# Queries and keys projected in transposed form, with the rotary halves swapped by DMA

## The chip, the cores and the metric

The kernel runs on one core of a Trainium2 chip. The metric is the device time of one execution in microseconds. The engines are TensorE (PE, matmuls; its weight loads are shown apart as PEld), VectorE (DVE), ScalarE (ACT), GpSimd (POOL) and SyncE (SP, which only issues DMAs here). SBUF is the on-chip memory of 128 partitions, PSUM the small memory that PE writes.

## The reference

Four stages on 16 sequences of 256 tokens with 128 features, all in float32: a state-space layer, a mixture of experts, a second state-space layer, and a transformer of six layers. The change lies in the transformer's attention:

```python
qkv = x @ Wqkv                      # shift_tokens(x): half of the features come from the token before
q, k, v = jnp.split(qkv, 3, -1)     # 16 heads of 64
q = l2norm(q) * qs
k = l2norm(k) * ksc
q = q * cos * scale + rotate_half(q) * sin * scale     # rotate_half: [-x2, x1] of the two halves of a head
k = k * cos / scale + rotate_half(k) * sin / scale
out = local_attention(q, k, v)      # windows of 32 tokens; each looks at itself and the one before
out = out @ Wo
```

After it come a residual add, a layer norm and a feed-forward layer with a GELU.

## The kernel before

The transformer phase (`transformer_phase`) works on 96 pieces: 6 layers times 16 sequences, numbered n. It is a software pipeline with an order written out by hand. A pass m handles five pieces at once, in different stages: A = m is projected, rotated and its norms taken, R = m - 1 is normalised and turned and its values are projected, B = m - 2 does scores, softmax and attention, Dn = m - 3 finishes attention and its output projection (`combine`), C = m - 4 does the feed-forward part. F is the final norm of the last 16 pieces. Each engine has its own list of steps for a pass, in program order; semaphores join them. An engine that waits holds up everything behind it in its list, and the same goes for SP's queue of DMAs.

Queries and keys of a piece are four units u of 128x1024 float32: u // 2 says queries or keys, u % 2 which half of the tokens; j = 4n + u. In the kernel before:
- PE, `project(n, u)`: tokens on partitions, 1024 features (16 heads x 64) along the free axis, into PSUM tile `pQ`.
- ACT, `square`: squares of `pQ` into `sq`. DVE, `squares`: a sum over the 64 of each head, into `n2`.
- DVE, `rotate`: `rot` = pQ times the cosine table (L1364), `m2` = pQ with its halves swapped by the access pattern times the sine table (L1368). The tables `tabl` are rebuilt once a layer from `tab` and `rows` (L1330).
- DVE, `roots`: the reciprocal root of 64 sums per partition, an instruction at L1386 and then eleven small ones of 128x64 (L92 to L102).
- POOL, `rotary_add` (L1282): rot += m2. `unit_scale` (L1274): rot times the reciprocal root. `by_sum` (L1291): softmax probabilities times the reciprocal sum.
- PE, `turn` (L1707): eight 128x128 transposes of `rot` into the two PSUM banks `pM`. ACT, `turned`: copies to `qT` and `kT`, where the features are on partitions.
- PE, `scores` (L1634), `probs` (L1664), `attend` (L1683), `values` (L1718), `combine` (L1696), `hidden` (L1752).

POOL can't read PSUM here, so it works on SBUF alone. The ring `rot` has five buffers. A float32 matmul is two instructions on PE; a transpose is one. The experts' phase has two large products, on DVE (L639) and on POOL (L570).

## Time and profile before

| | |
|---|---|
| median of 3 runs | 4262.65 us (4262.21 to 4263.87) |
| profiled execution | 4261.88 us, its span 4260.1 us |
| busy: PE, DVE, ACT, POOL | 4080.9, 3309.8, 2401.9, 2222.1 us |
| mean granted PE clock | 0.985 of full |
| all DMAs | 186.16 MB, 44 GB/s in the mean |

The span is the time from the first to the last instruction in the profile. Busy times of different engines overlap. The transformer phase runs from about 980 us to the end.

### The profile page before, as it was taken

The page shows a single profiled execution, that of the slowest core. Times are in us where ns is not written, and L with a number is a line of the kernel's source. Part 1 is how long each engine was busy: PE and PEld are TensorE (multiplying, and loading weights), DVE is VectorE, ACT ScalarE, POOL GpSimd, SP SyncE. Part 2 cuts the span into 40 slices and gives each one's busy share as a digit, 9 for nine tenths or more (in the row PEclk, how much of TensorE's full clock was granted, in tenths as well). Part 3 has the DMA queues.
Part 4 walks back from the last instruction along what each step waited for, and adds up shares of the span by engine and source line. Part 5 has one row for each costly group of instructions (what it writes and reads, how often), then busy time and mean ns, then how long its engine had stood idle before and what let it go on. Part 6 is the DMA issues. An engine that isn't in the chain of part 4 may idle for free.

```text
span 4260.1 us, 144544 instructions
## 1 busy us (share of the span) xinstructions
PE 4080.9 (96%) x63655; PEld 2975.2 (70%) x63655; DVE 3309.8 (78%) x7007; ACT 2401.9 (56%) x4362; POOL 2222.1 (52%) x1342
## 2 busy tenths in 40 slices
PE   4999999886999999999999999999999999999997
PEld 3776776673777777777777777777777777777775
DVE  5434434456888888888888888888888888889995
ACT  1101110144677766777667766776767677666664
POOL 1101001025666666666666666666666666666662
PEclk8999999998999999999999999999999999999998
DMA  4111111000111111111111111111111111111110
GB/s 153 42 40 60 40 40 60 20 1 24 36 36 41 42 56 41 40 38 45 51 42 41 37 44 52 41 41 37 46 50 41 41 37 51 46 43 41 43 40 25
DMA packets 76231, 186.16 MB, mean 44 GB/s; under 512 B 15819, under 2 KB 44630, under 8 KB 71126
## 3 DMA queue, kind: packets, MB, share of 16 engines
q1 hardware_dynamic: 75606, 176.91, 13.5%
q8 instruction: 504, 8.26, 0.8%
q14 instruction: 121, 0.99, 0.1%
HBM read 61.25 MB, written 2.36 MB: 15 GB/s over the span
## 4 chain that ended last, share of the span: by engine, by line
PE 66%; DVE 5%; ACT 3%; issue 1%; POOL 1%; DMA 0%; POOLq 0%; DVEq 0%; SPq 0%
PE pQ L1650 15%; PE pTO L1683 9%; PE pS L1634 9%; PE pM L1718 7%; PE pTO L1696 7%; PE pM L1707 7%; PE pC L1752 6%; PE pTO L1664 3%; PE pC L1762 3%; ACT sq L1515 2%; ACT pS L1499 1%; DVE rot L1364 1%; DVE m L1368 1%; DVE n L1379 1%; POOL rot L1282 1%
## 5 line engine op out<-in xcount | busy, mean ns | idle before, releaser
L1282 POOL TENSOR_TENSOR rot<-rot,m 128x1024 f32<-128x1024 f32 x384 | 905.9, 2359 | 385.6 <-DVE m L1368 385.6
L1274 POOL TENSOR_TENSOR rot<-rot,rn 128x1024 f32<-128x1024 f32 x384 | 733.4, 1910 | 280.7 <-DVE rn L102 280.7
L1515 ACT ACTIVATE sq<-pQ 128x1024 f32<-128x1024 f32 x380 | 389.4, 1025 | 440.0 <-PE pQ L1650 439.8
L1291 POOL TENSOR_TENSOR E<-E,rc 128x512 f32<-128x512 f32 x384 | 401.3, 1045 | 348.0 <-DVE rc L1354 347.9
L1683 PEld LDWEIGHTS pTO<-PT,V 64*64 64x64 f32 x24576 | 402.3, 134 | 108.8 <-issue 100.1
L1364 DVE TENSOR_TENSOR rot<-pQ,tabl 128x1024 f32<-128x1024 f32 x380 | 457.0, 1203 | 12.5 <-ACT sq L1515 9.9
L1368 DVE TENSOR_TENSOR m<-pQ,tabl 128x1024 f32<-128x1024 f32 x380 | 461.5, 1215 | 0.1
L1634 PEld LDWEIGHTS pS<-kT,qT 64*32 64x32 f32 x24576 | 362.0, 107 | 142.1 <-issue 107.7
L1379 DVE TENSOR_REDUCE n<-sq 128x16 f32<-128x1024 f32 x380 | 459.4, 1209 | 0.0
L1634 PE MATMUL pS<-kT,qT 64*32 64x64 f32 x24576 | 427.2, 218 | 26.4 <-issue 16.9
L1683 PE MATMUL pTO<-PT,V 64*64 64x32 f32 x24576 | 444.4, 221 | 3.9 <-ACT PT L1524 2.5
L1707 PE MATMUL pM<-ident,rot 128*128 128x128 f32 x3072 | 416.7, 279 | 18.0 <-POOL rot L1274 13.5
L570 POOL TENSOR_TENSOR b_xcT<-b_cB,b_xT 128x2048 f32<-128x2048 f32 x16 | 72.3, 4517 | 691.8 <-DMA b_cB<-b_crow 691.8
L1532 ACT ACTIVATE oT<-pTO 128x256 f32<-128x256 f32 x768 | 252.7, 381 | 262.1 <-PE pTO L1683 262.0
L1650 PE MATMUL pQ<-wq,xs 128*128 128x512 f32 x760 | 380.3, 623 | 6.3 <-DVE m L1368 5.6
L1718 PE MATMUL pM<-wv,xs 128*128 128x512 f32 x768 | 362.3, 594 | 3.4 <-ACT XT L1486 3.4
L1707 PEld LDWEIGHTS pM<-ident,rot 128*128 128x128 f32 x3072 | 332.7, 141 | 38.8 <-POOL rot L1274 16.7
L1650 PE MATMUL pQ<-wk,xs 128*128 128x512 f32 x760 | 357.2, 592 | 0.8 <-DVE m L1368 0.8
L1696 PE MATMUL pTO<-oT,wo 128*128 128x256 f32 x1536 | 350.0, 381 | 0.6 <-ACT oT L1532 0.4
L1340 DVE TENSOR_REDUCE mx<-pS 128x8 f32<-128x512 f32 x384 | 262.7, 684 | 72.4 <-PE pS L1634 72.2
L1696 PEld LDWEIGHTS pTO<-oT,wo 128*128 128x128 f32 x1536 | 286.1, 191 | 37.0 <-ACT oT L1532 1.2
L1752 PE MATMUL pC<-xnT,w 128*128 128x256 f32 x1152 | 299.6, 383 | 4.0 <-DVE hh L1420 2.2
(229 smaller groups left out, 6967.6 us busy)
## 6 DMA issues: line engine op xcount, KB each, us to landing
V<-V SPq DMA_DIRECT2D x192, 384.0 KB, 3.5
b_cB<-b_crow SPq DMA_DIRECT2D x32, 1024.0 KB, 6.4
xs<-XT SPq DMA_DIRECT2D x192, 64.0 KB, 2.9
V<-V SPq DMA_DIRECT2D x96, 128.0 KB, 3.3
ys<-XT SPq DMA_DIRECT2D x192, 64.0 KB, 2.0
wq<-in_wqkv SPq DMA_DIRECT2D x6, 512.0 KB, 4.3
wk<-in_wqkv SPq DMA_DIRECT2D x6, 512.0 KB, 4.2
wv<-in_wqkv SPq DMA_DIRECT2D x6, 512.0 KB, 5.5
```

The costliest lines, as they stand in the source:

```text
L1274: e.tensor_tensor(r, r, rn[b % 2][:, c:c + HEADS].unsqueeze(2).to_broadcast([P, HEADS, HD]), ALU.mult)\
L1282: e.tensor_tensor(rot[j % RING][:, :], rot[j % RING][:, :], m2[:, :, :].rearrange("p h d -> p (h d)"), ALU.add)\
L1364: e.tensor_tensor(rot[j % RING][:, :].rearrange("p (h d) -> p h d", d=HD), projected(j)[:, :].rearrange("p (h d) -> p h d", d=HD), tl[:, t ...
L1368: e.tensor_tensor(m2[:, :, :].rearrange("p h (b d) -> p h b d", b=2), projected(j)[:, :].rearrange("p (h b d) -> p h b d", b=2, d=HD // 2) ...
L1379: e.tensor_reduce(n2[:, c:c + HEADS], squared(j).rearrange("p (h d) -> p h d", d=HD), AX.X, ALU.add)\
L1634: x = e.matmul(pS[32 * j:32 * j + 32, b * KEYS:(b + 1) * KEYS], q[r:r + HD, h // 2, WIN * w:WIN * (w + 1)], k[r:r + HD, h // 2, WIN * w:WI ...
L1650: x = e.matmul(projected(j)[:, i * 512:(i + 1) * 512], xs[n % 3][:, t * P:(t + 1) * P], wqkv[w][:, i * 512:(i + 1) * 512], start=True, sto ...
L1683: x = e.matmul(pOV[b % 2][c:c + HD, j // 2, w // 4, WIN * (w % 2):WIN * (w % 2 + 1)], V[n % 2][r:r + KEYS, w // 4, 1 - w % 2, h * HD:(h + ...
L1696: x = e.matmul(pO[:, 0:L], wo[:, c, :], oT[:, c, :], start=c == 0, stop=c == N // P - 1)
L1707: x = e.transpose(pM[i][:, c * P:(c + 1) * P], rot[j % RING][:, (4 * i + c) * P:(4 * i + c + 1) * P], ident[:, :])
L1718: e.matmul(pM[i][:, :], xs[n % 3][:, t * P:(t + 1) * P], wqkv[2][:, i * 512:(i + 1) * 512], start=True, stop=True)\
L1752: x = e.matmul(pC[:, a * L:(a + 1) * L], w1[:, c, :], xnT[:, :], start=True, stop=True)
```

## The change

Queries and keys are projected with the features on partitions and the 256 tokens along the free axis. A unit is now u // 2 = queries or keys and u % 2 = which eight heads, as four blocks of 128 features x 256 tokens. The transposes and their copies out of PSUM go away. In their place:
- ACT copies the unit from `pQ` to `rot` (`copied`), besides squaring it.
- Swapping the two halves of a head now means moving partitions: four DMAs on SP's queue (`swap`) copy `rot` to `rsw`, 32 partitions x 4 KB each.
- DVE multiplies `rot` by the cosine table in place (`cosine`) and `rsw` by the sine table in place (`sine`); POOL adds them as before.
- The sums of squares run over partitions, so PE takes them with a matrix of zeros and ones (`norms`, `sel`): 16 matmuls of 128x32 weights by 64 columns for a unit, into four 32-partition strips of the new PSUM tile `pN`. The matrix gives the 64 sums per partition a new layout.
- The reciprocal roots go to device memory (`write_rows`, `nrow`) and come back spread over partitions (`spread`, two DMAs of 64 partitions x 4 KB for a unit) into `rb`, and POOL's `unit_scale` multiplies `rot` by `rb`, writing to `qT` and `kT`.
- `pM` is one bank. The tables are transposed on PE at the start of the phase and their plain form is kept in device memory (`plain`), to be fetched again for each layer. `rot` has six buffers. The lists of all engines are reordered.

The diff, cut to its core:

```diff
-    RING = 5
+    RING = 6
...
+        plain = nc.dram_tensor("plain", (P, 4 * L), F32).ap()
+        tabl = [sb("tabl0", [P, 4 * L])[:, :], tab[:, :, :, :, :].rearrange("p t k i d -> p (t k i d)")]
+        tabl = [x.rearrange("p (k l) -> p k l", k=4) for x in tabl]
+        sel = sb("sel", [P, 16 * 32])
...
+        rb = [sb(f"rb{i}", [P, 4, L]) for i in range(2)]
+        nrow = [nc.dram_tensor(f"nrow{i}", (P, L // 4), F32).ap() for i in range(2)]
+        rsw = [sb(f"rsw{i}", [P, N]) for i in range(2)]
...
-        pM = [ps("pM0", [P, 512]), ps("pM1", [P, 512])]
+        pM = ps("pM", [P, 512])
+        pN = ps("pN", [P, 512])
...
+            def swap(n, u):
+                if n is None:
+                    return
+                j = 4 * n + u
+                e.wait_ge(a_raw.sem, a_raw.at("cp", j))
+                if j >= 2:
+                    e.wait_ge(g_add.sem, g_add.at("add", j - 2))
+                for a in range(4):
+                    b = a ^ 1
+                    e.dma_start(rsw[j % 2][a * HD // 2:(a + 1) * HD // 2, :], rot[j % RING][b * HD // 2:(b + 1) * HD // 2, :])\
+                        .then_inc(swap_l[j % 2], 16)
...
+            def write_rows(n):
+                if n is None:
+                    return
+                e.wait_ge(v_nt.sem, v_nt.at("rs", n))
+                if n >= 2:
+                    for i in range(2):
+                        e.wait_ge(rb_l[i], 32 * (2 * n - 3))
+                e.dma_start(nrow[n % 2], rn[n % 2][:, :]).then_inc(row_l, 16)
+            def spread(n, u):
+                if n is None or n == NP and u < 2 or n == 0 and u >= 2:
+                    return
+                i = 4 * (n - u // 2) + u
+                e.wait_ge(row_l, 16 * (n + 1))
+                if i >= 2:
+                    e.wait_ge(g_rn.sem, g_rn.at("rn", i - 2))
+                for x in range(2):
+                    src = nrow[n % 2].rearrange("(j i x) k -> i j (x k)", j=4, i=2)[x:x + 1, :, u * L:(u + 1) * L]
+                    e.dma_start(rb[u % 2][x * HD:(x + 1) * HD, :, :], src.to_broadcast([HD, 4, L])).then_inc(rb_l[u % 2], 16)
...
+                swap(A, 0)
+                N_ = A if A is not None else NP if R == NP - 1 else None
+                next_xs(A)
+                ffn_weights(C)
+                swap(A, 1)
+                write_rows(N_)
+                swap(A, 2)
+                spread(N_, 2)
+                spread(N_, 3)
+                next_ys(Dn)
+                swap(A, 3)
+                spread(N_, 0)
+                spread(N_, 1)
+                shift_values(R, 0)
+                store(F)
+                shift_values(R, 1)
...
-                b, c = n + u // 2, (u + 2) % 4 * HEADS
-                if u % 2 == 0:
-                    e.wait_ge(v_nt.sem, v_nt.at("rs", b))
+                e.wait_ge(rb_l[u % 2], 32 * (2 * n + u // 2 + 1))
+                if u % 2 == 0 and n >= 2:
+                    e.wait_ge(p_s.sem, p_s.at("s", 4 * (n - 2) + 3))
                 e.wait_ge(g_add.sem, g_add.at("add", j))
-                r = rot[j % RING][:, :].rearrange("p (h d) -> p h d", d=HD)
-                e.tensor_tensor(r, r, rn[b % 2][:, c:c + HEADS].unsqueeze(2).to_broadcast([P, HEADS, HD]), ALU.mult)\
+                a = 4 * (u % 2)
+                dst = (kT[n % 2][:, a:a + 4, WIN:] if u // 2 else qT[n % 2][:, a:a + 4, :])
+                e.tensor_tensor(dst, rot[j % RING][:, :].rearrange("p (j l) -> p j l", l=L), rb[u % 2][:, :, :], ALU.mult)\
                     .then_inc(g_rn.sem, 1)
             def rotary_add(n, u):
                 if n is None:
                     return
                 j = 4 * n + u
-                e.wait_ge(v_rot.sem, v_rot.at("sin", j))
-                e.tensor_tensor(rot[j % RING][:, :], rot[j % RING][:, :], m2[:, :, :].rearrange("p h d -> p (h d)"), ALU.add)\
-                    .then_inc(g_add.sem, 1)
+                e.wait_ge(v_cos.sem, v_cos.at("cos", j))
+                e.wait_ge(v_sin.sem, v_sin.at("sin", j))
+                e.tensor_tensor(rot[j % RING][:, :], rot[j % RING][:, :], rsw[j % 2][:, :], ALU.add).then_inc(g_add.sem, 1)
...
                 unit_scale(R, 0)
                 root(C)
+                by_sum(B, 0)
+                by_sum(B, 1)
                 rotary_add(A, 0)
                 unit_scale(R, 1)
-                by_sum(B, 0)
                 rotary_add(A, 1)
+                by_sum(B, 2)
                 unit_scale(R, 2)
+                unit_scale(R, 3)
                 last_root(F)
-                by_sum(B, 1)
-                unit_scale(R, 3)
+                by_sum(B, 3)
                 rotary_add(A, 2)
-                by_sum(B, 2)
-                by_sum(B, 3)
...
-            def rotate(n, u):
-                if n is None:
-                    return
-                j, w, t = 4 * n + u, u // 2, u % 2
-                tl = tabl[n // NSEQ % 2]
-                e.wait_ge(a_sq.sem, a_sq.at("sq", j))
-                if j >= RING:
-                    e.wait_ge(p_tr.sem, p_tr.at("b", j - RING))
-                e.tensor_tensor(rot[j % RING][:, :].rearrange("p (h d) -> p h d", d=HD), projected(j)[:, :].rearrange("p (h d) -> p h d", d=HD),
-                                tl[:, t, 2 * w, :].unsqueeze(1).to_broadcast([P, HEADS, HD]), ALU.mult).then_inc(v_rot.sem, 1)
-                if j:
-                    e.wait_ge(g_add.sem, g_add.at("add", j - 1))
-                e.tensor_tensor(m2[:, :, :].rearrange("p h (b d) -> p h b d", b=2),
-                                projected(j)[:, :].rearrange("p (h b d) -> p h b d", b=2, d=HD // 2)[:, :, ::-1, :],
-                                tl[:, t, 2 * w + 1, :].rearrange("p (b d) -> p b d", b=2).unsqueeze(1).to_broadcast([P, HEADS, 2, HD // 2]),
-                                ALU.mult).then_inc(v_rot.sem, 1)
-            def squares(n, u):
-                if n is None:
-                    return
-                j, c = 4 * n + u, (u + 2) % 4 * HEADS
-                if u == 2:
-                    e.wait_ge(v_nt.sem, v_nt.at("rs", n))
-                e.tensor_reduce(n2[:, c:c + HEADS], squared(j).rearrange("p (h d) -> p h d", d=HD), AX.X, ALU.add)\
-                    .then_inc(v_red.sem, 1)
+            def cosine(n, u):
+                if n is None:
+                    return
+                j = 4 * n + u
+                e.wait_ge(swap_l[j % 2], 64 * (j // 2 + 1))
+                x = rot[j % RING][:, :].rearrange("p (j l) -> p j l", l=L)
+                e.tensor_tensor(x, x, tabl[n // NSEQ % 2][:, 2 * (u // 2), :].unsqueeze(1).to_broadcast([P, 4, L]), ALU.mult)\
+                    .then_inc(v_cos.sem, 1)
+            def sine(n, u):
+                if n is None:
+                    return
+                j = 4 * n + u
+                e.wait_ge(swap_l[j % 2], 64 * (j // 2 + 1))
+                x = rsw[j % 2][:, :].rearrange("p (j l) -> p j l", l=L)
+                e.tensor_tensor(x, x, tabl[n // NSEQ % 2][:, 2 * (u // 2) + 1, :].unsqueeze(1).to_broadcast([P, 4, L]), ALU.mult)\
+                    .then_inc(v_sin.sem, 1)
             def roots(n):
                 if n is None:
                     return
-                e.wait_ge(v_red.sem, v_red.at("rd", 4 * n + 1 if n < NP else 4 * n - 1))
-                e.tensor_scalar(n2[:, :], n2[:, :], 1e-24, None, ALU.max).then_inc(v_nt.sem, 1)
+                e.wait_ge(p_n.sem, p_n.at("n", 4 * n + 1 if n < NP else 4 * n - 1))
+                if n >= 2:
+                    e.wait_ge(row_l, 16 * (n - 1))
+                e.tensor_scalar(n2[:, :], pN[:, 0:L // 4], 1e-24, None, ALU.max).then_inc(v_nt.sem, 1)
...
                 less_max(B, 0)
                 statistics(C)
-                rotate(A, 0)
+                sums(B, 0)
+                less_max(B, 1)
                 normal(C)
-                squares(A, 0)
-                less_max(B, 1)
-                sums(B, 0)
-                rotate(A, 1)
-                squares(A, 1)
+                cosine(A, 0)
+                sums(B, 1)
+                sine(A, 0)
+                attention_add(Dn)
                 roots(A if A is not None else NP if R == NP - 1 else None)
-                last_stats(F)
-                attention_add(Dn)
                 less_max(B, 2)
-                sums(B, 1)
                 hidden(C, 0)
-                rotate(A, 2)
-                less_max(B, 3)
-                squares(A, 2)
-                last_normal(F)
+                sine(A, 1)
+                cosine(A, 1)
                 sums(B, 2)
                 hidden(C, 1)
+                last_stats(F)
                 hidden(C, 2)
+                less_max(B, 3)
+                sine(A, 2)
                 sums(B, 3)
-                rotate(A, 3)
                 ffn_add(C)
-                squares(A, 3)
+                cosine(A, 2)
+                sine(A, 3)
+                last_normal(F)
+                cosine(A, 3)
...
+            def copied(n, u):
+                if n is None:
+                    return
+                j = 4 * n + u
+                e.wait_ge(p_q.sem, p_q.at("q", j))
+                if j >= RING:
+                    e.wait_ge(g_rn.sem, g_rn.at("rn", j - RING))
+                e.activation(rot[j % RING][:, :], projected(j)[:, :], ACT.Copy).then_inc(a_raw.sem, 1)
...
-                for i in range(2):
-                    x = e.matmul(projected(j)[:, i * 512:(i + 1) * 512], xs[n % 3][:, t * P:(t + 1) * P], wqkv[w][:, i * 512:(i + 1) * 512],
-                                 start=True, stop=True)
+                    e.wait_ge(a_raw.sem, a_raw.at("cp", before(j)))
+                    e.wait_ge(a_sq.sem, a_sq.at("sq", before(j)))
+                for i in range(4):
+                    c = 4 * t + i
+                    x = e.matmul(projected(j)[:, i * L:(i + 1) * L], wqkv[w][:, c * P:(c + 1) * P], xs[n % 3][:, 0:L], start=True, stop=True)
...
-            def turn(n, u):
+            def norms(n, u):
                 if n is None:
                     return
                 j = 4 * n + u
-                e.wait_ge(g_rn.sem, g_rn.at("rn", j))
-                for i, half in enumerate("ab"):
-                    free(i)
-                    for c in range(4):
-                        x = e.transpose(pM[i][:, c * P:(c + 1) * P], rot[j % RING][:, (4 * i + c) * P:(4 * i + c + 1) * P], ident[:, :])
-                    x.then_inc(p_tr.sem, 1)
-                    bank[i] = (a_tr, half, j)
-            def values(n, t):
-                if n is None:
-                    return
-                if t == 0 and starts(n):
+                e.wait_ge(a_sq.sem, a_sq.at("sq", j))
+                if u == 2:
+                    e.wait_ge(v_nt.sem, v_nt.at("mn", n))
+                for b in range(4):
+                    for i in range(4):
+                        x = e.matmul(pN[32 * i:32 * i + 32, 0:L // 4], sel[:, 32 * (4 * u + b):32 * (4 * u + b + 1)],
+                                     squared(j)[:, i * L + b * L // 4:i * L + (b + 1) * L // 4], start=(b == 0 and (u == 2 or j == 0)),
+                                     stop=((u == 1 or j == 4 * NP - 1) and b == 3), skip_group_check=True, tile_position=(0, 32 * i))
+                x.then_inc(p_n.sem, 1)
...
-                scores(B, 0)
                 project(A, 0)
                 back(C)
                 probs(Dn, 3)
-                turn(R, 0)
+                scores(B, 0)
+                norms(A, 0)
+                attend(Dn, 3)
+                values(R, 0)
+                project(A, 1)
                 scores(B, 1)
-                attend(Dn, 3)
-                project(A, 1)
-                values(R, 0)
+                combine(Dn)
                 normed(C)
-                combine(Dn)
                 probs(B, 0)
+                norms(A, 1)
                 hidden(C, 0)
-                last(F)
                 project(A, 2)
                 scores(B, 2)
-                turn(R, 1)
                 hidden(C, 1)
                 attend(B, 0)
-                turn(R, 2)
-                scores(B, 3)
-                probs(B, 1)
                 values(R, 1)
                 project(A, 3)
+                probs(B, 1)
                 hidden(C, 2)
+                norms(A, 2)
+                last(F)
+                scores(B, 3)
                 attend(B, 1)
-                turn(R, 3)
+                values(R, 2)
+                contract(C)
                 probs(B, 2)
-                contract(C)
+                norms(A, 3)
+                values(R, 3)
                 attend(B, 2)
```

## Rows read from the trace of the kernel before

**Rows 1.** The page, chain of work that ended last, shares of the span by engine
```profile
PE 66%; DVE 5%; ACT 3%; issue 1%; POOL 1%; DMA 0%; POOLq 0%; DVEq 0%; SPq 0%
```

**Rows 2.** Busy time by stretch: stretch, length, engines, PE clock, DMA share, GB/s
```profile
2000.00:3500.00 1500.00, 1488.34 (x28074) 1084.59 (x28067) 1329.89 (x2397) 1051.75 (x1898) 983.23 (x587) 1.00 0.15 43
```

**Rows 3.** Line 1386 from 2000 to 3500 us: count, min/median/max ns, first and last start
```profile
L1386 DVE TENSOR_SCALAR n<-n x45: 1320/1326/1337, 2008.5 to 3470.2; 128x64 f32<-128x64 f32 x45
```

**Rows 4.** Timeline of PE: start us, us from first start to last end, line, instructions
```profile
2004.92 3.62 PE L1696 MATMUL pTO<-oT,wo 128*128 128x256 f32 x16
...
2009.68 1.88 PE L1650 MATMUL pQ<-wk,xs 128*128 128x512 f32 x4
...
2011.49 1.10 PE L1634 MATMUL pS<-kT,qT 64*32 64x64 f32 x64
...
2012.52 1.09 PE L1707 MATMUL pM<-ident,rot 128*128 128x128 f32 x8
...
2013.45 1.03 PE L1752 MATMUL pC<-xnT,w 128*128 128x256 f32 x4
```

**Rows 5.** Groups by shape, 2000 to 2343.6 us: busy us, mean ns, idle before
```profile
L1282 POOL TENSOR_TENSOR rot<-rot,m 128x1024 f32<-128x1024 f32 x42 | 99.1, 2359 | 40.2 <-DVE m L1368 40.2
...
L1274 POOL TENSOR_TENSOR rot<-rot,rn 128x1024 f32<-128x1024 f32 x41 | 78.5, 1915 | 29.3 <-DVE rn L102 29.3
...
L1291 POOL TENSOR_TENSOR E<-E,rc 128x512 f32<-128x512 f32 x41 | 42.8, 1045 | 35.3 <-DVE rc L1354 35.3
...
L1379 DVE TENSOR_REDUCE n<-sq 128x16 f32<-128x1024 f32 x42 | 50.8, 1209 | 0.0
...
L1515 ACT ACTIVATE sq<-pQ 128x1024 f32<-128x1024 f32 x41 | 42.0, 1025 | 46.7 <-PE pQ L1650 46.7
```

**Rows 6.** The page, costliest groups: busy us, mean ns, idle before
```profile
L570 POOL TENSOR_TENSOR b_xcT<-b_cB,b_xT 128x2048 f32<-128x2048 f32 x16 | 72.3, 4517 | 691.8 <-DMA b_cB<-b_crow 691.8
```

**Rows 7.** Single lines: count, min/median/max ns, first and last start
```profile
L1330 DVE TENSOR_TENSOR tabl<-tab,rows x6: 694/1505/1512, 980.8 to 3621.6; 128x512 f32<-128x512 f32 x6
...
L639 DVE TENSOR_TENSOR b_xcT<-b_cB,b_xT x16: 2281/3279/5294, 105.3 to 784.7; 128x2048 f32<-128x2048 f32 x16
...
L1364 DVE TENSOR_TENSOR rot<-pQ,tabl x181: 1180/1212/1225, 2005.0 to 3499.7; 128x1024 f32<-128x1024 f32 x181
```

**Rows 8.** Timelines of DVE and POOL where they meet
```profile
2026.56 2.36 POOL L1282 TENSOR_TENSOR rot<-rot,m 128x1024 f32<-128x1024 f32 x1 [1.19 <-DVE m L1368]
...
2028.88 2.35 POOL L1274 TENSOR_TENSOR rot<-rot,rn 128x1024 f32<-128x1024 f32 x1
...
2027.96 1.50 DVE L1330 TENSOR_TENSOR tabl<-tab,rows 128x512 f32<-128x512 f32 x1
...
2041.41 2.35 POOL L1282 TENSOR_TENSOR rot<-rot,m 128x1024 f32<-128x1024 f32 x1 [1.00 <-DVE m L1368]
...
2042.49 1.32 DVE L1386 TENSOR_SCALAR n<-n 128x64 f32<-128x64 f32 x1
```

**Rows 9.** Timeline of DVE after the root's first instruction
```profile
2043.84 0.20 DVE L92 TENSOR_SCALAR rn<-n 128x64 int32<-128x64 int32 x1
...
2046.53 0.42 DVE L1394 TENSOR_TENSOR XT<-pTO,XT 128x256 f32<-128x256 f32 x1
...
2046.86 0.68 DVE L1340 TENSOR_REDUCE mx<-pS 128x8 f32<-128x512 f32 x1
...
2048.25 0.68 DVE L1352 TENSOR_REDUCE sm<-E 128x8 f32<-128x512 f32 x1
...
2049.11 0.48 DVE L1420 SCALAR_TENSOR_TENSOR hh<-pC,vec,hh 128x256 f32<-128x256 f32 x1
...
2049.51 1.22 DVE L1364 TENSOR_TENSOR rot<-pQ,tabl 128x1024 f32<-128x1024 f32 x1
```

**Rows 10.** Timeline of the DMA issues on SP's queue
```profile
2040.51 0.60 SPq L1234 DMA_DIRECT2D V<-V  x1
```

**Rows 11.** DMA issues, 2000 to 3500 us: KB each, median us to landing
```profile
V<-V SPq DMA_DIRECT2D x45, 128.0 KB, 3.3
```

More of the change, by code:

```diff
@@ L192, in __init__ @@
         self.b2r = sb("b2r", [DEPTH, D])
-        self.rows = sb("rows", [P, DEPTH, 4 * HD])
-        self.tab = sb("tab", [P, T, 4 * HD])
+        self.rows = sb("rows", [P, DEPTH, 4])
+        self.tab = sb("tab", [P, T, 4, 2, HD])
         self.mask = sb("mask", [P, NW * KEYS])
@@ L1219, in _, with store @@
+            def store(n):
+                if n is None:
+                    return
+                f = n - (NP - NSEQ)
+                e.wait_ge(v_f.sem, v_f.at("out", f))
+                e.dma_start(out[:, f, :, :], X[:, f, :, :]).then_inc(stored, 16)
             fetch_xs(0)
+            e.wait_ge(v_set, 3)
+            e.dma_start(plain.rearrange("p (k l) -> p k l", k=4), tabl[1]).then_inc(plain_l, 16)
+            e.wait_ge(plain_l, 16)
             for A, R, B, Dn, C, F in passes():
-                if A is not None and A + 1 < NP:
-                    fetch_xs(A + 1)
@@ L1435, in last_stats @@
                 xv = X[:, f, :, :].rearrange("p t d -> p (t d)")
-                e.tensor_tensor(xv, xv, pM[0][:, 0:L], ALU.add).then_inc(v_f.sem, 1)
+                e.tensor_tensor(xv, xv, pM[:, 0:L], ALU.add).then_inc(v_f.sem, 1)
                 e.wait_ge(v_f.sem, v_f.at("add", f))
```

219 lines of the change are left out of this document (122 added, 97 removed).

## The prediction

> **What bounds the kernel now.** I read the page first: the chain of work that ended last lies on TensorE (PE) for 66% of the span, on VectorE (DVE) for 5% [rows 1]. Then the steady stretch of the transformer phase by engine [rows 2]: PE is busy for 1488 of 1500 us, DVE 1330, ScalarE (ACT) 1052, GpSimd (POOL) 983, at a granted clock of 1.00. Then the length of a pass: the first instruction of `roots` comes once in each, 45 times from 2008.5 to 3470.2 [rows 3], so a pass is 1461.7 / 44 = 33.2 us. 96 of them make 3190 of the 4260 us; ahead of this phase the diff changes only a few loads. A pass holds 1488 / 1500 x 33.2 = 33.0 us of PE and 29.4 of DVE. PE paces it and DVE has 4 us in hand.
>
> **What goes, PE.** The 32 transposes of `turn`: a batch of eight takes 0.93 us from start to start [rows 4], four take 3.7. `project` computes as many columns as before, in 32 instructions of 256 instead of 16 of 512. Today's four for a unit take 1.81 us, 7.2 a pass; `combine` issues 16 of 128x256 in 3.62 [rows 4], so 32 cost 7.2. Nothing gained or lost.
>
> **What comes, PE.** `norms`: per unit 16 matmuls, that is 32 instructions, of 64 moving columns, into one of four 32-column groups of the array. No row has a tile of 128 rows x 32 columns. The nearest is `scores`: 64 instructions of 64 columns that rotate through four column groups, in 1.03 us [rows 4]: 16.1 ns each, so 0.52 per unit and 2.1 us a pass. If the four groups don't overlap, each costs half of a 128-column instruction of `turn` (0.93 / 8 / 2 = 0.058), 7.4 a pass. I take 2.1, since `scores` rotates in the same way, and keep 7.4 for the range. PE then needs 33.0 - 3.7 + 2.1 = 31.4 us, at most 36.7.
> The Trainium skill (TensorE: Matmul & The Clock Gate, Wait — 56ns, not 53.3ns?) says that matmuls never start less than about 25 ns apart, however small. The 16.1 ns of `scores` go against it, so the measurement decides; by it norms would cost 3.2 us, and PE still would not pace the pass that I forecast.
>
> **What goes and comes, DVE and ACT.** The four reductions of squares go, 4 x 1.21 = 4.8 us [rows 5]. The eight products with the tables and the root's small instructions stay. On ACT eight copies of 128x512 become four of 128x1024, the same elements, on an engine that is 70% busy [rows 2]: nothing. Counted alone, DVE falls to 24.6 us and PE to 31.4, and the pass would be 31.4.
>
> **But the products change what they read.** Today each takes one operand from PSUM (`pQ`) and one from SBUF, and runs through POOL's work unhurt: 1180 to 1225 ns over 181 of them [rows 7]. After, both come from SBUF (`rot` or `rsw`, and `tabl`). The trace shows what that means. The one instruction of this phase with two large SBUF operands, `tabl<-tab,rows`, takes 694 ns alone and 1505 when POOL works [rows 7]: it starts at 2027.96, POOL's add ends at 28.92, and it ends at 29.46. POOL's next product, from 28.88, takes 2.35 us instead of 1.91 [rows 5, 8]. The experts' phase has one too, 2281 ns at the least, 3279 in the median and 5294 at most [rows 7]. And the root's first instruction, SBUF to SBUF with 64 elements, takes 1326 [rows 3]: it starts at 2042.49 and ends at 43.81, just after POOL's add at 43.76 [rows 8]. So the two engines don't run such instructions side by side: each waits for the other's current one, as at a door.
>
> What must go through that door in a pass, from durations, overlaps of 0.04 left out:
> - `rotary_add`, 4 x 2.32 = 9.3 [rows 5].
> - `unit_scale`, today 1.91, with its second operand broadcast along 64 elements [rows 5]. After, both are dense over 1024. Nearest: POOL's `b_xcT`, 4517 ns for 2048 elements [rows 6], 2.26 per 1024; bounds 1.91 and the add's 2.36. I take 2.26: 9.0.
> - `by_sum`, 4 x 1.05 = 4.2 [rows 5], and the power, some 0.7.
> - `cosine` and `sine`, eight. POOL lost 0.44 us to a 512-wide one, 0.9 per 1024; the whole duration is 1.21. I take 1.05 between them: 8.4.
>
> That is 31.6 us. To it come the times in which neither uses the door, because of the written order. One: `by_sum(B,1)` waits for `sums(B,1)`, which stands behind `cosine(A,0)`: 0.9 [rows 9]. The larger: while POOL does `rotary_add(A,0)` and `unit_scale(R,1)`, DVE is in `roots`. Its small SBUF instructions get through one or two at a time between POOL's, so most of the chain (2.4 of 2.7 us [rows 9]) runs after `unit_scale(R,1)`. POOL's next item, `rotary_add(A,1)`, needs `sine(A,1)` and `cosine(A,1)`, and these stand on DVE behind `roots`, `less_max(B,2)` (1.4) and `hidden(C,0)` (0.4) [rows 9]: 4.2 us with POOL idle. From there to the next pass's `by_sum(B,0)` there is always a POOL instruction or a DVE product at the door, and `normal(C)`, `sums` and the rest wait behind them. The pass is 31.6 + 0.9 + 4.2 = 36.7 us: +3.5.
> The Trainium skill (SBUF — State Buffer, SBUF: two separate sides) has this as an exclusive lock on a port pair that both engines share, held for the whole instruction. The trace agrees that the other one blocks. Taken at its word, the eight products would cost 9.7 us and not 8.4, and the pass would be 38.0.
>
> **What is hidden.** The new DMAs, behind the pass itself. SP issues 32 a pass instead of 7, at 0.6 us each [rows 10], 19 us. The cover is thin at one place: `write_rows` waits on SP for `roots`, and `swap(A,2)` and the spreads for units 2 and 3 are queued behind it. From the end of `roots`: 0.6 for the row, 2.4 for four swap issues, 3.3 to land [rows 11] is 6.3, and DVE comes to `sine(A,2)` after 1.4 + 0.4 + 2.4 + 0.9 + 0.8 + 1.4 = 7.3. For `unit_scale(R,2)`: the row lands at 3.9, its spread is issued at 5.1 and lands at 8.4, and POOL wants it after 4.2 + 2.3 + 1.05 = 7.6. Some 0.8 late, but DVE's `sine(A,2)` can use the door then; I charge nothing and keep up to 1.5 us as a rival. Without that cover, late swaps would hold DVE, and behind it everything. The other new waits (the ring of `rot`, `rsw` freed by the add of two units before, `pN`, one `pM` instead of two, `project` behind two ACT passes over `pQ` instead of one and two DVE products) end earlier than what I have named. Once only, the plain tables go to memory ahead of the first pass: 0.6 + 3.3, some 4 us.
>
> **The sum.** The profiled execution took 4261.9 us for a span of 4260.1; the median of the runs is 4262.65, 0.8 above it. 4261.9 + 96 x 3.5 + 4 = 4602; rounded down for the bounds, which reach further down than up, 4590.
> Its own range: `unit_scale` at 1.91 and the products at 0.9 give 34.1 us, 4350; the add's 2.36 and 1.21 give 38.4, 4765. Not both at once: 4420 to 4720.
>
> **Rivals.**
> 1. Faster (0.16). DVE and POOL find each other's gaps, the root's chain isn't split, and PE paces on at 31.4: 4262 - 96 x 1.8 = 4090, half way 4170. It decides if door and idle together stay under 33.2. For it: the door's lower bound is 29.9 (1.91 and 0.9). Against: 5 us of idle follow from the written order.
> 2. The blocking is there but mild (0.15): lower prices and half the idle, 33.2 to 35 us, 4262 to 4435; of this 0.04 for no difference and 0.01 for a hair faster.
> 3. The DMAs come late as well (0.12): `unit_scale(R,2)` or a swap 1.5 us late in each pass, on the chain: 4590 + 145 = 4735, and more if issue times stretch.
> 4. PE paces after all (0.05): norms without overlap, 36.7 us in place of the door and not on top of it, 4600, and less in part overlap.
> The forecast has 0.52. Faster is 0.17; same 0.04 (within 0.2%, some 8 us, about what a measurement of this kernel can tell); slower 0.79. The range leaves out rival 1 and the far end of 3: 4300 to 4760.
>
> **What the next profile would show.** PE at some 31 us a pass with gaps, norms at 16 ns an instruction. `cosine` and `sine` at 1.8 us or more in the mean, spread from 1.2 to 3.5, and small instructions of `roots` of 2 us among those of 0.2. `unit_scale` at 2.3. A chain that runs over DVE and POOL. If the products take 1.2 us each while POOL works beside them, the step on the door is wrong and rival 1 holds. If `unit_scale` or the products wait for DMAs for long, it is rival 3.

## The result and the profile after

The changed kernel takes 5324.5 us in the median of 4 runs (5312.4 to 5333.2), the kernel before 4262.4 beside it (4260.0 to 4263.9): 1.249 times, with an interval of 1.2474 to 1.2512. That is +1062 us. The forecast was +328; the direction is right, the size is not, and the time lies outside the range. The times of the experiments are medians of four runs each, but one run of n4 (14055.7 us at a granted clock of 0.27) and one of n7 (6882.2 us at 0.58) were far slower than their fellows, and without them the medians are 4744.4 us for n4, used here where the later expectations say 4747, and 4604.6 for n7.

The page of the kernel after: busy time, DMA queues, chain of waits, the costliest groups, and DMA issues with their landing times. They answer to [rows 1, 5, 7, 11].
```profile
span 5331.4 us, 169240 instructions
PE 4420.7 (83%) x74415; PEld 3371.4 (63%) x74415; DVE 3508.0 (66%) x6624; ACT 2415.0 (45%) x3978; POOL 2650.3 (50%) x1344
...
q1 hardware_dynamic: 377846, 585.00, 47.0%
q8 instruction: 588, 9.63, 0.8%
...
DVE 28%; PE 22%; issue 15%; POOL 13%; DMA 2%; SPq 1%; ACT 0%; DVEq 0%; POOLq 0%
...
L1369 POOL TENSOR_TENSOR rot<-rot,rsw 128x1024 f32<-128x1024 f32 x384 | 987.6, 2577 | 689.2 <-DVE rot L1455 670.5
L1377 POOL TENSOR_TENSOR E<-E,rc 128x512 f32<-128x512 f32 x384 | 533.0, 1388 | 759.0 <-DVE rc L1447 758.5
...
L1360 POOL TENSOR_TENSOR kT<-rot,rb 128x1024 f32<-128x1024 f32 x192 | 494.3, 2582 | 319.9 <-DMA rb<-nrow 318.1
...
L1464 DVE TENSOR_TENSOR rsw<-rsw,tabl 128x1024 f32<-128x1024 f32 x192 | 274.0, 1427 | 211.3 <-DMA rsw<-rot 211.3
...
rsw<-rot SPq DMA_DIRECT2D x1536, 128.0 KB, 4.0
rb<-nrow SPq DMA_DIRECT2D x768, 256.0 KB, 6.5
V<-V SPq DMA_DIRECT2D x192, 384.0 KB, 7.3
...
V<-V SPq DMA_DIRECT2D x96, 128.0 KB, 7.2
```
PE was 66% of the chain before [rows 1] and is 22% now. DVE and POOL have 41% of it together, as forecast. The forecast has no place for two others: 15% is "issue", in which an engine waits for nothing that the profile shows, and the landing times have doubled, 7.2 us for the shift of 128 KB where [rows 11] has 3.3. Queue 1 moves 585 MB, three times as much as before.

The first instruction of `roots`, once a pass, and the windows of the kernel after (PE, PE loads, DVE, ACT, POOL busy, then the granted clock, the DMA share and GB/s):
```profile
L1473 DVE TENSOR_SCALAR n<-pN x45: 210/214/225, 2531.2 to 4482.8; 128x64 f32<-128x64 f32 x45
```
```profile
2000.00:4000.00 2000.00, 1642.69 (x33108) 1267.98 (x33106) 1410.48 (x2210) 1057.95 (x1716) 1181.29 (x588) 0.90 0.57 129
3043.00:3046.00 3.00, 0.18 (x13) 0.07 (x6) 2.90 (x4) 0.00 (x0) 1.84 (x2) 0.99 0.99 251
3046.00:3049.30 3.30, 0.05 (x5) 0.05 (x4) 0.94 (x6) 0.00 (x0) 3.30 (x2) 0.50 1.02 222
```
A pass is (4482.8 - 2531.2) / 44 = 44.4 us; it was 33.2 [rows 3] and 36.7 was forecast. The DMA engines are busy for 57% in the mean, 15% before [rows 2], and for 99% or more in both short windows.

The waits of the kernel after from 2000 to 4000 us, 45 passes: who waits for whom, us in total, times, longest.
```profile
DVE rsw L1464 <- DMA rsw<-rot: 188.7, 45, 7.9
...
PE pTO L1780 <- issue: 164.4, 62, 6.8
...
POOL kT L1360 <- DMA rb<-nrow: 147.8, 56, 4.9
```
Per pass, DVE waits 4.2 us for swapped halves, POOL 3.3 us for spread roots, and PE 3.7 us in the middle of `attend` for nothing that is named.

The timeline of the kernel after in the pass around 3016, the door (start, length, engine, line), and around 3040, where PE stops:
```profile
3016.73 2.40 POOL L1369 TENSOR_TENSOR rot<-rot,rsw 128x1024 f32<-128x1024 f32 x1
...
3016.85 2.34 DVE L95 TENSOR_SCALAR rn<-rn 128x64 int32<-128x64 int32 x1
...
3019.10 2.36 POOL L1360 TENSOR_TENSOR qT<-rot,rb 128x1024 f32<-128x1024 f32 x1
3019.23 2.31 DVE L98 TENSOR_TENSOR rt<-rn 128x64 f32<-128x64 f32 x1
...
3039.29 2.04 DVE L1464 TENSOR_TENSOR rsw<-rsw,tabl 128x1024 f32<-128x1024 f32 x1 [2.25 <-DMA rsw<-rot]
3040.21 3.35 POOL L1369 TENSOR_TENSOR rot<-rot,rsw 128x1024 f32<-128x1024 f32 x1
...
3041.25 3.38 DVE L1455 TENSOR_TENSOR rot<-rot,tabl 128x1024 f32<-128x1024 f32 x1
```
```profile
3042.50 0.68 PE L1780 MATMUL pTO<-PT,V 64*64 64x32 f32 x31
3049.25 1.10 PE L1780 MATMUL pTO<-PT,V 64*64 64x32 f32 x33 [6.07 <-issue]
```
The first part is the door as the prediction drew it: two instructions of 128x64, which take 0.2 us elsewhere, take 2.34 and 2.31 because they end with POOL's. The second is what it did not have. `attend` is one run of 64 instructions on the same operands. PE stops after 31 of them for 6.07 us while the DMA engines are full. In the window over the first half of that stop its granted clock is 0.99, in the window over the second half 0.50, the 1.2 GHz level.

### The profile page after: what moved, and what is told of

Its sections match the earlier page's. It is cut to its first block, busy times and chain, and to the rows that moved or that the text cites. A ratio compares the mean times of both kernels' runs of the same rounds, so it can differ in the third digit from the quotient of the medians.

```text
span 5331.4 us, 169240 instructions
## 1 busy us (share of the span) xinstructions
PE 4420.7 (83%) x74415; PEld 3371.4 (63%) x74415; DVE 3508.0 (66%) x6624; ACT 2415.0 (45%) x3978; POOL 2650.3 (50%) x1344
## 4 chain that ended last, share of the span: by engine, by line
DVE 28%; PE 22%; issue 15%; POOL 13%; DMA 2%; SPq 1%; ACT 0%; DVEq 0%; POOLq 0%
POOL kT L1360 8%; PE pQ L1748 5%; PE pS L1730 5%; DVE rt L98 5%; POOL E L1377 4%; DVE rn L95 4%; DVE rsw L1464 4%; DVE rot L1455 4%; PE pTO L1780 4%; PE pM L1817 4%; DVE E L1437 2%; DVE mx L1433 2%; PE pN L1805 2%; PE pTO L1761 2%; POOL rot L1369 1%
## 5 line engine op out<-in xcount | busy, mean ns | idle before, releaser
L1369 POOL TENSOR_TENSOR rot<-rot,rsw 128x1024 f32<-128x1024 f32 x384 | 987.6, 2577 | 689.2 <-DVE rot L1455 670.5
L1360 POOL TENSOR_TENSOR kT<-rot,rb 128x1024 f32<-128x1024 f32 x192 | 494.3, 2582 | 319.9 <-DMA rb<-nrow 318.1
L1445 DVE TENSOR_REDUCE sm<-E 128x8 f32<-128x512 f32 x384 | 261.2, 680 | 336.5 <-ACT E L1594 335.9
L1748 PE MATMUL pQ<-xs,wq 128*128 128x256 f32 x1520 | 458.1, 454 | 7.3 <-issue 7.3
L1761 PE MATMUL pTO<-ident,E 128*128 128x128 f32 x1536 | 258.0, 295 | 235.2 <-POOL E L1377 233.3
L1360 POOL TENSOR_TENSOR qT<-rot,rb 128x1024 f32<-128x1024 f32 x192 | 451.3, 2350 | 0.0
L1748 PEld LDWEIGHTS pQ<-xs,wq 128*128 128x128 f32 x1520 | 349.6, 235 | 152.6 <-issue 96.9
L1612 ACT ACTIVATE rot<-pQ 128x1024 f32<-128x1024 f32 x380 | 388.3, 1022 | 59.9 <-PE pQ L1748 42.9
L1464 DVE TENSOR_TENSOR rsw<-rsw,tabl 128x1024 f32<-128x1024 f32 x192 | 274.0, 1427 | 211.3 <-DMA rsw<-rot 211.3
L1464 DVE TENSOR_TENSOR rsw<-rsw,tab 128x1024 f32<-128x1024 f32 x192 | 268.8, 1400 | 169.6 <-DMA rsw<-rot 169.6
```

The costliest lines, as they stand in the source:

```text
L1360: e.tensor_tensor(dst, rot[j % RING][:, :].rearrange("p (j l) -> p j l", l=L), rb[u % 2][:, :, :], ALU.mult)\
L1369: e.tensor_tensor(rot[j % RING][:, :], rot[j % RING][:, :], rsw[j % 2][:, :], ALU.add).then_inc(g_add.sem, 1)
L1464: e.tensor_tensor(x, x, tabl[n // NSEQ % 2][:, 2 * (u // 2) + 1, :].unsqueeze(1).to_broadcast([P, 4, L]), ALU.mult)\
L1612: e.activation(rot[j % RING][:, :], projected(j)[:, :], ACT.Copy).then_inc(a_raw.sem, 1)
L1748: x = e.matmul(projected(j)[:, i * L:(i + 1) * L], wqkv[w][:, c * P:(c + 1) * P], xs[n % 3][:, 0:L], start=True, stop=True)
L1761: x = e.transpose(pT[:, b * P:(b + 1) * P], E[i % 2][:, b * P:(b + 1) * P], ident[:, :])
```

## The experiments

They were compared with the kernel before on the same chip, whose median was 4262.4 to 4265.2. First, each suspect of the prediction was taken out of the changed kernel: the DMAs (n1), the door at the products (n2), both (n3), the spreads alone (n4).

**n1, no DMAs.** The swap, row and spread DMAs are gone; `rsw` starts as zeros and `rb` as ones, so halves are not swapped and nothing is normalised. All instructions of the engines stay.
```diff
-                for a in range(4):
-                    b = a ^ 1
-                    e.dma_start(rsw[j % 2][a * HD // 2:(a + 1) * HD // 2, :], rot[j % RING][b * HD // 2:(b + 1) * HD // 2, :])\
-                        .then_inc(swap_l[j % 2], 16)
...
-                e.wait_ge(swap_l[j % 2], 64 * (j // 2 + 1))
+                e.wait_ge(a_raw.sem, a_raw.at("cp", j))
```


> The changed kernel (5324 us) without its new data transfers: no half-swap DMAs (rsw holds zeros, set once), no row writes and no spreads (rb holds ones, set once); all products, adds and unit_scale stay, each waiting for the copy or the roots that its data came from. It leaves out the swap of halves and the norms. Theory D (the DMA traffic makes its own data late and holds up what else comes over the DMA engines, the instructions of TensorE among them): the pass falls from 44.4 us to the door's 36.7 of the prediction or less, 4600 us in all, 4450 to 4700, and TensorE's stops inside attend, up to 6 us long, vanish. Theory P (the 11 us a pass are the mutual blocking of VectorE and GpSimd over two-input SBUF instructions, which is dearer than I priced it): 5100 us or more.

4728.3 us, 1.109 (1.1072 to 1.1109), just above the 4450 to 4700 of theory D. The DMAs are worth 596 us, more than half of the loss. What is left, 466 us over the kernel before, lies at the door and in PE's own list, which n3 and n8 take apart.

**n2, products kept away from the door.** Each product becomes a sum over the same 128x1024 tile, of like duration (1.21 us) but with one SBUF input; rotation is left out.
```diff
-                e.tensor_tensor(x, x, tabl[n // NSEQ % 2][:, 2 * (u // 2), :].unsqueeze(1).to_broadcast([P, 4, L]), ALU.mult)\
-                    .then_inc(v_cos.sem, 1)
+                e.tensor_reduce(dm[:, HEADS * (2 * (j % 6) + 0):HEADS * (2 * (j % 6) + 1)], rot[j % RING][:, :].rearrange("p (h d) -> p h d", d=HD), AX.X, ALU.add).then_inc(v_cos.sem, 1)
```


> The changed kernel with its eight table products a pass replaced by reductions of the same 128x1024 tile, same length (1.21 us), one SBUF input, so that they need no door; all DMAs stay. It leaves out the products. Theory D: little gained, 5100 to 5300 us. Theory P: it gives back most, under 4700 us.

5206.8 us, 1.221 (1.2186 to 1.2232), within the 5100 to 5300 of theory D. Only 118 us come back.

**n3, both edits.** It leaves out what n1 and n2 leave out.

> Both edits of the two others together: no swap, row and spread DMAs, and reductions in place of the products. Both theories: TensorE paces again, at 31.4 us a pass as in the prediction's sum for TensorE, 4090 us; if it stays above 4262, something else than DMAs and the door costs, e.g. TensorE's own new work.

4387.8 us, 1.029 (1.0275 to 1.0310), where 4090 was expected: something else costs as well, which n8 takes up. Without the DMAs the same opening of the door is worth 4728.3 - 4387.8 = 340 us, against 118 with them. The likely reason, which no run isolates, is that engines that wait for data anyway lose less at the door.

**n4, swaps kept, rows and spreads left out** (`rb` holds ones).
```diff
-                e.dma_start(nrow[n % 2], rn[n % 2][:, :]).then_inc(row_l, 16)
...
-                for x in range(2):
-                    src = nrow[n % 2].rearrange("(j i x) k -> i j (x k)", j=4, i=2)[x:x + 1, :, u * L:(u + 1) * L]
-                    e.dma_start(rb[u % 2][x * HD:(x + 1) * HD, :, :], src.to_broadcast([HD, 4, L])).then_inc(rb_l[u % 2], 16)
```


> The changed kernel without row writes and spreads (rb holds ones, set once; unit_scale waits for the roots), with the swap DMAs. It leaves out the norms. The spreads are half of the new bytes but 224 thousand of 378 thousand packets (1 KB each), and sit in SP's queue between swaps. Theory D: half or more of what the run without both DMAs gives back, 4800 to 5000 us. Theory P: under 100 us gained.

4744.4 us, 1.113 (1.1110 to 1.1154), 16 us over n1 and below the 4800 to 5000 that was expected. Its new transfers land so:
```profile
rsw<-rot SPq DMA_DIRECT2D x1536, 128.0 KB, 2.4
```
The sixteen swap DMAs of a pass cost almost nothing. Nearly all of the 596 us comes with the spreads.

The next runs ask whether the spreads cost by the wait for their data or by their traffic (n5, n6), whether traffic alone slows the kernel before (n7, n11, n12), and what the door takes from n3 still (n8).

**n5, spreads that nobody reads.** The DMAs are issued from the same places; `unit_scale` waits only for `roots` and multiplies `rot` by itself, so nothing is normalised. Since `unit_scale` no longer waits for a spread, SP does in its place: it issues one only when the spread of two units before has landed (23 us of waiting from 2000 to 4000). **n6** is n5 with each spread read as one run of 4 KB instead of four runs of 1 KB: the same bytes in other packets.
```diff
-                e.wait_ge(rb_l[u % 2], 32 * (2 * n + u // 2 + 1))
+                e.wait_ge(v_nt.sem, v_nt.at("rs", n + u // 2))
...
-                    src = nrow[n % 2].rearrange("(j i x) k -> i j (x k)", j=4, i=2)[x:x + 1, :, u * L:(u + 1) * L]
-                    e.dma_start(rb[u % 2][x * HD:(x + 1) * HD, :, :], src.to_broadcast([HD, 4, L])).then_inc(rb_l[u % 2], 16)
+                    src = nrow[n % 2].rearrange("(u i y) k -> (u i) (y k)", u=4, i=2)[2 * u + x:2 * u + x + 1, :]
+                    e.dma_start(rb[u % 2][x * HD:(x + 1) * HD, :, :].rearrange("p j l -> p (j l)"), src.to_broadcast([HD, 4 * L])).then_inc(rb_l[u % 2], 16)
```


> The changed kernel (5324 us; 4747 without spreads) with every DMA still issued from the same place in SP's queue, but nobody waits for a spread: unit_scale waits for the roots only and multiplies rot by itself (two dense SBUF inputs as before). It leaves out the norms. Theory L (the spread costs because its data come late for unit_scale): 4750 to 4850 us. Theory Q (the traffic itself costs, by holding up swaps, value shifts and the DMAs that bring TensorE its instructions): 5100 to 5300, with TensorE's stops without a visible cause still some 4 us a pass.

> As the run with unread spreads, but each spread reads 4 KB in one piece per partition instead of four of 1 KB, from the same rows: same bytes, a quarter of the packets. If the number of packets is what costs: near 4750 us. If it is the bytes in a burst: like the run with unread spreads, within 100 us.

n5: 5082.1 us, 1.193 (1.1902 to 1.1957). n6: 4766.9 us, 1.120 (1.1165 to 1.1231). Queue 1 and the waits, first of n5, then of n6:
```profile
q1 hardware_dynamic: 377846, 585.00, 49.4%
...
DVE rsw L1466 <- DMA rsw<-rot: 201.6, 47, 7.5
PE pTO L1782 <- issue: 182.8, 66, 6.7
```
```profile
q1 hardware_dynamic: 230390, 585.00, 49.9%
...
DVE rsw L1466 <- DMA rsw<-rot: 115.1, 47, 5.3
PE pTO L1782 <- issue: 112.4, 58, 4.4
```
The bytes are equal and the shares of the DMA engines nearly so. With 147,000 packets fewer the time falls by 315 us, and so do both waits. n6 is 22 us above n4, which has no spreads at all. Both came out close to what theory Q and the count of packets said (5100 to 5300, and near 4750). Waiting for the spread data itself, as the changed kernel does, costs 5324.5 - 5082.1 = 242 us.

**n8, n3 with the door wide open.** The twelve small instructions behind the first of `roots` (L92, L93, L95 and three times L98, L100, L102 of the helper; there are twelve in the kernel before as well, not eleven), of which three average 2.0, 1.7 and 0.9 us in n3, become sums with one SBUF input too (the reciprocal root is left out).
```diff
-                vector_rsqrt(e, v_nt, n, "rs", rn[n % 2][:, :], n2[:, :], rh[:, :], rt[:, :])
+                for k in range(VRS):
+                    e.wait_ge(v_nt.sem, v_nt.at("rs", n, VRS - k))
+                    e.tensor_reduce(rn[n % 2][:, k:k + 1], n2[:, :], AX.X, ALU.add).then_inc(v_nt.sem, 1)
```


> The changed kernel without its DMAs and with reductions for the products (4388 us), and the root's twelve later instructions replaced by as many reductions of 64 elements with one SBUF input, so that no VectorE work of the change meets GpSimd at the door. It leaves out swap, products and norms. If the split root chain is what keeps this kernel 125 us above the one before: 4250 to 4310. If TensorE's own list is (its busy time is 32.9 us a pass there, not 31.4): 4360 or more.

4206.7 us, 0.987 (0.9848 to 0.9890), below both of the expected ranges. The chain of waits, the window and the first instruction of `roots` of n3, then of n8:
```profile
PE 39%; DVE 31%; issue 4%; POOL 1%; DMA 1%; ACT 1%; SPq 0%; DVEq 0%; POOLq 0%; ACTq 0%
...
2000.00:4000.00 2000.00, 1916.26 (x42215) 1499.83 (x42215) 1649.97 (x2845) 1340.00 (x2185) 1346.65 (x747) 0.98 0.16 43
...
L1462 DVE TENSOR_SCALAR n<-pN x58: 214/216/218, 2004.0 to 3986.8; 128x64 f32<-128x64 f32 x58
```
```profile
PE 72%; DVE 2%; issue 1%; ACT 1%; DMA 0%; POOL 0%; SPq 0%; POOLq 0%; DVEq 0%; ACTq 0%
...
2000.00:4000.00 2000.00, 1977.94 (x44747) 1568.20 (x44746) 1521.34 (x3048) 1417.31 (x2314) 1437.74 (x799) 1.00 0.17 46
...
L1462 DVE TENSOR_SCALAR n<-pN x61: 212/215/216, 2016.5 to 3987.3; 128x64 f32<-128x64 f32 x61
```
A pass of n3 is (3986.8 - 2004.0) / 57 = 34.8 us, one of n8 (3987.3 - 2016.5) / 60 = 32.8. The small instructions alone are worth 181 us. With them gone PE paces, as in rival 1, but at 4207 us and not 4090.

**n7, n11, n12, the kernel before with traffic that nobody reads.** SP issues in each pass the sixteen swap-like DMAs (n12), the eight spread-like ones (n11) or both (n7), between SBUF tiles and a row of device memory that the kernel doesn't use. Shown is n7 at two of its places:
```diff
             for A, R, B, Dn, C, F in passes():
+                swap()
                 if A is not None and A + 1 < NP:
                     fetch_xs(A + 1)
...
+                swap()
+                spread(2)
+                spread(3)
                 if Dn is not None:
```


> The kernel before (4262 us) plus DMAs of the size and number of the change on SP's queue: per pass 16 as the swaps and 8 as the spreads, between tiles that nothing else uses, waited for by nobody but the next of them. All the computation is in it. Theory Q: slower by 300 us or more, with stops of several us of TensorE inside attend or scores that no engine or data explains. Theory L: within 60 us of 4262.

> The kernel before with the 8 spread-like DMAs a pass alone (256 KB each, pieces of 1 KB), read by nobody: most of the 342 us that both kinds of traffic cost it, 200 to 330.

> The kernel before with the 16 swap-like DMAs a pass alone (128 KB each, pieces of 4 KB), read by nobody: 0 to 60 us, like the 19 us between the two changed kernels with and without swaps.

n7: 4604.6 us, 1.078 (1.0741 to 1.0814), +342. n11: 4355.0 us, 1.021 (1.0194 to 1.0228), +90, under the 200 to 330 that I expected. n12: 4286.7 us, 1.005 (1.0036 to 1.0069), +21. The waits of n7, then of the kernel before, from 2000 to 4000:
```profile
PE pS L1671 <- issue: 100.7, 52, 6.8
```
```profile
PE pS L1634 <- issue: 12.0, 13, 1.3
```
Their windows in the same order:
```profile
2000.00:4000.00 2000.00, 1870.37 (x33984) 1347.91 (x33983) 1617.52 (x2897) 1278.32 (x2296) 1188.42 (x712) 0.97 0.63 154
```
```profile
2000.00:4000.00 2000.00, 1979.91 (x37285) 1442.51 (x37280) 1778.68 (x3232) 1397.19 (x2519) 1309.33 (x786) 1.00 0.15 44
```
No engine of n7 reads the added data, and still PE stops in the middle of `scores`, for up to 6.8 us. The stops aren't all of the 342 us: PE is idle for 130 of 2000 us against 20 before, which is 2.4 us of a pass against 0.3, some 195 us in all. PE's busy time per pass also grows, from 33.0 to 34.2 us, at a granted clock of 0.97 instead of 1.00. The two kinds of traffic cost more together (342) than apart (111). n9 and n10 are two tries at a version worth having.

**n9, the whole change with spreads of 4 KB.** Two small DMAs from device memory to device memory sort the rows by unit first, so that the spreads of n6 read right values.
```diff
+                e.wait_ge(row_l, 48 * n + 16)
+                for i in range(2):
+                    e.dma_start(urow[n % 2].rearrange("(u i j x) k -> i j u (x k)", u=4, i=2, j=4)[i],
+                                nrow[n % 2].rearrange("(j i u x) k -> i j u (x k)", u=4, i=2, j=4)[i]).then_inc(row_l, 16)
```


> The changed kernel, complete, with the spreads read in pieces of 4 KB: the rows go to device memory as now (pieces of 256 B), two DMAs within device memory sort them by unit (64 pieces of 1 KB), and each spread reads 4 KB per partition in one piece. Three DMAs more in SP's queue, two waits for landings in it, a quarter of the packets in the spreads. If the packets are the cost, as 5082 against 4767 said: 4780 to 4950 us against 5324. If the lateness of the rows costs as much as it saves: above 5100.

5176.0 us, 1.213 (1.2089 to 1.2161), where 4780 to 4950 was expected. The waits of n9, 2000 to 4000:
```profile
DVE rsw L1469 <- DMA rsw<-rot: 310.8, 93, 8.5
...
POOL kT L1365 <- DMA rb<-urow: 213.3, 67, 6.9
...
PE pC L1835 <- DMA ys<-XT: 75.8, 39, 4.0
...
PE pTO L1785 <- issue: 61.6, 51, 3.5
```
PE's stops fall as in n6, from 164 us to 62. But SP now waits for the row and then for the sort, with `swap(A, 2)` and the fetch of `ys` queued behind, and DVE's wait for swaps rises from 189 us to 311 and POOL's for roots from 148 to 213.

**n10, n9 and the products read PSUM again.** `cosine` and `sine` take `pQ`, and the product with the sine is swapped, not the raw copy. The copy on ACT is gone; the lists of SP, POOL and DVE are reordered.
```diff
-                    e.dma_start(rsw[j % 2][a * HD // 2:(a + 1) * HD // 2, :], rot[j % RING][b * HD // 2:(b + 1) * HD // 2, :])\
+                    e.dma_start(rsw[j % 2][a * HD // 2:(a + 1) * HD // 2, :], yn[b * HD // 2:(b + 1) * HD // 2, :])\
```


> The version before, complete, with both products reading pQ in PSUM again, so that they need no door: the sine product is made first, with its table's halves exchanged, and the DMAs swap the halves of the product; ACT's copies go, the ring has 5 buffers, and the lists of VectorE, GpSimd and SP are reordered for it. From the runs: the door was worth 340 us and the 4 KB pieces 400 or more, so 4350 to 4600; below 4262 only if the lists fit much better than I expect.

5690.0 us, 1.335 (1.3322 to 1.3367), the worst of all, where 4350 to 4600 was expected. Its largest wait for a DMA, 2000 to 4000:
```profile
POOL kT L1366 <- DMA rb<-urow: 478.4, 42, 13.9
```
Opening the door didn't help here. Swaps now follow DVE's work instead of ACT's. Roots, row, sort and spread follow one another in SP's queue, and POOL waits 11 us a pass at their end with its whole list behind it. Its order was reworked in several places at once, so the size of each part isn't separated.

## Why the prediction was right on the door and wrong on the time

The runs make a ladder. Each step is a difference of two medians, some of them from different chips, on which the kernel before differed by up to 3 us. The runs of one kernel lie 5 to 32 us apart, so the two steps of 16 and 22 us say little more than that they are small:

| from | to | us | what it adds |
|---|---|---|---|
| before 4262 | n8 4207 | -56 | the change on PE, with neither door nor DMAs |
| n8 | n3 4388 | +181 | the small instructions of `roots` at the door |
| n3 | n1 4728 | +340 | the eight products at the door |
| n1 | n4 4744 | +16 | the swaps |
| n4 | n6 4767 | +22 | unread spreads in 4 KB packets |
| n6 | n5 5082 | +315 | the same bytes in 1 KB packets |
| n5 | after 5324 | +242 | the wait for the spread data |

**The door: the mechanism was right, and the size with some luck.** The step from PE's own pass (31.4 us) to that of the door with its idle time (36.7) was 5.3 us, 509 us in all. Measured are 181 + 340 = 521. The total agrees better than its parts. The largest part of the forecast idle time, a root chain cut up by POOL's instructions, was 4.2 us a pass, 403 us; the step that removes that chain is 181. In n1 from 2000 to 4000, by the trace's records, POOL or one of the eight products is busy for 31.9 us of a pass, where the door's sum was 31.6, and neither is for 6.4, where 5.1 was forecast: 38.4 us, not 36.7. `unit_scale` takes 2.35 for `qT` (forecast 2.26), and with the waits for `kT` 2.58, in n1 3.3. That the products would show 1.8 us or more was off: they take 1.40 to 1.64 in the mean, and 1.63 to 1.84 in n1. The lower figures of the changed kernel fit its late data, which move products to times when POOL isn't at work; no run isolates this. In rival 1 the lower bound of the door, 29.9, is 29.0 by its own rows (9.3 + 7.6 + 4.2 + 0.7 + 7.2), which changes nothing in the sum.
The Trainium skill (SBUF — State Buffer, Who interferes with whom) says that a DVE instruction with two SBUF inputs contends with a GpSimd instruction that reads SBUF, and one with at most one SBUF input, outside certain fast modes, doesn't. n2 and n3 agree: with one large input, DVE's sums take 1.21 and POOL's `by_sum` is back at 1.04.

**PE: right sign, gain too large.** Free of the rest, PE gives 4207 us (n8) where 31.4 us a pass meant 4090. In the window of n8 PE is busy for 1977.9 of 2000 us, 32.5 of a pass of 32.8, at a granted clock of 1.00; in n3 it is 33.3 of 34.8. The step "PE then needs 33.0 - 3.7 + 2.1 = 31.4" was mis-sized by (4207 - 4090) / 96 = 1.2 us a pass. Two parts of it can be named. `norms` issues a unit in 0.59 us from start to start, not 0.52, which is 0.3 a pass. And `values`, for which the prediction counted no change ("one `pM` instead of two" ends "earlier than what I have named"), went from two blocks of four instructions, 1.72 us each, to four blocks of two on the one bank `pM`, 0.96 each: 0.4 a pass. Why its blocks take longer was not tested.

**The DMAs: the failed step.** The prediction said under "What is hidden": "The new DMAs, behind the pass itself", and "I charge nothing". They cost 596 us (the changed kernel against n1), 6.2 us a pass. The landing time in that working, 3.3 us, was read from a kernel whose DMA engines were busy for 15%. It held for the swaps alone, which land in 2.4 us in n4 and cost 16 us. Four spreads of 256 KB for two units, with shifts and swaps close behind them, fill all engines for several us (0.99 and more from 3043 to 3049.3). Then a swap lands in 4.0 us, a spread in 6.5, and the cover of 7.3 and 7.6 us that the prediction counted is gone. Rival 3 named this wait and priced it at 1.5 us a pass; the waits are 4.2 on DVE and 3.3 on POOL.

**And PE's own instructions come by the same engines.** The pages of both kernels list queue 8, kind "instruction", in packets of 16 KB, 588 in the kernel after. In its stretch from 2000 to 4000 I compared the packet records with PE's waits for "issue" of 0.5 us or more: all 82 of them, 195 us, end between 1.2 and 1.7 us after the end of such a packet. 7% of moments picked at random lie so. In n7 it is 66 of 66, 123 us, and in the kernel before 13 of 13, where they come to only 12.6 us. In n10 it is 29 of 70; the other 41 stand ahead of the first matmul of `attend`, which waits for semaphores, so "issue" in a profile isn't always a wait for instructions. The stop shown above ends at 3049.25; the packet's row was read in its window:
```profile
DMA packets 116, 0.38 MB, mean 222 GB/s; under 512 B 27, under 2 KB 27, under 8 KB 115
...
q8 instruction: 1, 0.02, 6.0%
```
That is 3046.2 to 3047.9, and PE goes on 1.4 us later. So I read these stops as PE running out of instructions when a block is late. That it is late because of data packets ahead of it is shown as far as n7 goes: traffic that nobody reads brings the stops about. n6 shows that fewer and longer packets ease it (PE's waits in `attend` 183 to 112 us).
The Trainium skill (DMA: Bandwidth & Descriptors, Queues, rings and completion order) has each DMA engine take its queues in turn and switch only after a whole packet, which there is some 9 to 17 descriptors. If one record of the profile is one such descriptor, which no run here shows, an estimate from that figure and the 276 ns of a 4 KB record is 2.5 to 4.7 us for one turn. The trace doesn't bear it out as it stands: by that rule shorter pieces would mean shorter turns, but PE's stops reach 6.7 us with pieces of 1 KB (n5) and 4.4 with 4 KB (n6). No run here shows where in between a block waits.

**What stays open.** Of the 315 us of packet size, how much is PE's late instructions and how much late swaps isn't separated, since one run changes both. Nor is the clock: PE is busy for 32.5 us a pass in n8 at a granted clock of 1.00, and for 36.4 in the changed kernel at 0.90, so part of what the table puts down to the door and the DMAs is PE working slower after its stops. The parts don't add up across orders either (the products are worth 340 us without DMAs and 118 with them), so the table is one path and not a list of prices. Why n11's spreads cost 90 us on the kernel before and the same spreads unread 338 in the changed one (n5 minus n4) is only argued: the kernel before spaces its other transfers wider and has no swaps to be late.

No version of the change came near the kernel before. n8, which has neither door nor DMAs and leaves out part of the work, is 1.3% under it: that is about what this form of the change could give, and against it stand 521 us at the door and 596 at the DMAs.

## What to carry to other kernels

A landing time holds only at the DMA load at which it was read: before hiding a transfer behind a pass, add up bytes and packets of the bursts that fall together, and see who waits in order behind each. Spreading a small row over many partitions is no small transfer: it moves the size of its target (here 2 MB a pass), and here pieces of 1 KB instead of 4 KB made that dearer by 315 us. And before an operand moves from PSUM to SBUF, list which DVE instructions will then meet GpSimd's, the small ones in a serial chain above all.

## What the runs showed of the hardware

- PE stops while the DMA engines are full of data that nobody reads (n7): up to 6.8 us in the middle of a run of equal matmuls, each ended by a 16 KB packet of the instruction queue some 1.2 to 1.7 us before. In the changed kernel the second half of a stop of 6.07 us has a granted clock of 0.50.
- At equal bytes (585 MB) and nearly equal DMA share (49.4 and 49.9%), spreads in pieces of 1 KB cost 315 us more than in pieces of 4 KB. In the changed kernel a 1 KB packet took 60 ns in the median, a 4 KB one 276.
- DVE and GpSimd exclude one another for single instructions of 128x64 too: 2.3 us instead of 0.2. A chain of twelve such instructions in a pass costs 181 us over 96 passes (n3 against n8).
- Sixteen transfers of 128 KB between partitions in each pass cost the kernel before 21 us (n12).
